# Cross-attention by pairs of token tiles, with maxima from stacked scores and a second, transposed score product

## What is computed

```python
q = einsum('bsd,hdk->bhsk', layernorm(x), Wq) + bq      # 16 heads, 16 wide
k, v = the same of ctx (2, 154, 256) with Wk, bk, Wv, bv
attn = softmax(q @ k.T / 4, axis=-1)                    # per head, 154 keys
x = x + concat(attn @ v) @ Wo + bo
logits = layernorm(x) @ router_w.T                      # 8 experts, the 2 best
x = x + sum over the 2 experts of w_e * gelu(xn @ w1[e].T) @ w2[e].T
```

## Time and profile before

| | us |
|---|---|
| median of 3 runs | 484.65 (482.76 to 489.57) |
| the profiled execution | 481.93, span 480.1 |
| PE busy | 421.6 (88%) |
| DVE, ACT, POOL busy | 327.6, 258.2, 259.8 |
| first scores of tile 0 | start at 17.78 |
| last logits copied (end of attention) | 207.45 |
| first expert product | starts at 236.93 |

### The profile page before, as it was taken

How to read it: one execution, slowest core, us unless ns; L and a number is a source line. 1 busy time by engine, 2 the same in 40 slices (tenths; PEclk the granted TensorE clock), 3 DMA queues, 4 the chain that set the end, 5 groups by cost and what they waited for, 6 DMA issues and landing times.

```text
span 480.1 us, 11162 instructions
## 1 busy us (share of the span) xinstructions
PE 421.6 (88%) x3421; PEld 373.5 (78%) x3422; DVE 327.6 (68%) x701; ACT 258.2 (54%) x509; POOL 259.8 (54%) x302
## 2 busy tenths in 40 slices
PE   7678999999999999722789999899999999999950
PEld 3467888888888887511489999899999999999940
DVE  1688999999999999569675755545446786664310
ACT  1555776677767775431076565454456767464410
POOL 2678778787777787410613364544544536462331
PEclk8999999999999999955799999999999999999995
DMA  8411111111111111075261734535324474232131
GB/s 235 143 40 46 57 56 67 56 77 65 55 55 61 59 56 67 23 202 173 58 259 48 219 56 122 132 51 128 50 42 129 90 223 91 39 59 34 24 38 12
DMA packets 24486, 41.98 MB, mean 87 GB/s; under 512 B 5952, under 2 KB 19136, under 8 KB 22400
## 3 DMA queue, kind: packets, MB, share of 16 engines
q1 hardware_dynamic: 13664, 28.68, 17.5%
q0 software_dynamic: 7296, 10.01, 12.2%
q10 hardware_dynamic: 3488, 2.83, 1.9%
HBM read 25.75 MB, written 9.45 MB: 73 GB/s over the span
## 4 chain that ended last, share of the span: by engine, by line
PE 73%; DVE 8%; DMA 7%; POOL 4%; issue 4%; ACT 1%; ACTq 1%; DVEq 0%; POOLq 0%
PE ps_s L1274 21%; PE ps_t L1291 13%; PE ps_s L1119 11%; PE ps_t L1294 7%; PE ps_t L1134 6%; PE ps_a L1152 3%; PE ps_c L1169 3%; DMA XS<-in_x 2%; PE ps_a L1075 2%; DMA result<-big,rowtok 2%; PE ps_a L1147 2%; DMA big<-rows,gtok 2%; PE ps_c L1256 2%; PE ps_c L1181 1%; PE ps_c L1175 1%
## 5 line engine op out<-in xcount | busy, mean ns | idle before, releaser
L488 POOL DMA_INDIRECT result<-big,rowtok x38 | 66.5, 1750 | 112.6 <-DMA result<-big,rowtok 63.2
L1274 PE MATMUL ps_s<-xgT,KB 128*128 128x256 f32 x912 | 116.0, 284 | 3.0 <-DVE xgT L999 3.0
L1274 PEld LDWEIGHTS ps_s<-xgT,KB 128*128 128x128 f32 x912 | 110.9, 191 | 4.1 <-DVE xgT L999 1.7
L1119 PE MATMUL ps_s<-KB 128*128 (+1 forms) x384 | 72.0, 324 | 9.4 <-DVE VP L756 3.2
L1119 PEld LDWEIGHTS ps_s<-KB 128*128 128x128 f32 x384 | 57.0, 193 | 14.3 <-issue 7.4
L456 POOL DMA_INDIRECT big<-rows,gtok x38 | 42.8, 1126 | 42.9 <-DVE gtok L976 23.7
L564 ACT ACTIVATE VP<-ps_t 128x512 f32<-128x512 f32 x80 | 47.5, 599 | 21.5 <-PE ps_t L1134 19.7
L393 POOL TENSOR_TENSOR half<-big 128x256 f32<-128x256 f32 x64 | 47.5, 742 | 16.2 <-ACT big L556 16.0
L1291 PE MATMUL ps_t<-KB,HTb 128*128 x160 | 56.0, 391 | 0.0
L646 ACT ACTIVATE big<-ps_t,wrow 128x256 f32<-128x256 f32 x38 | 18.1, 475 | 70.3 <-PE ps_t L1294 67.3
L1042 DVE SCALAR_TENSOR_TENSOR big<-ps_t,wrow,big 128x256 f32<-128x256 f32 x38 | 18.4, 483 | 52.4 <-ACT big L646 46.3
(11 more groups left out here) (159 smaller groups left out, 783.8 us busy)
## 6 DMA issues: line engine op xcount, KB each, us to landing
VP<-in_wexp SPq DMA_DIRECT2D x8, 1024.0 KB, 5.4
big<-in_wexp SPq DMA_DIRECT2D x8, 1024.0 KB
VP<-VP SPq DMA_DIRECT2D x16, 384.0 KB, 2.6
result<-x SPq DMA_DIRECT2D x16, 128.0 KB, 1.7
rows<-xn SPq DMA_DIRECT2D x16, 128.0 KB, 2.2
XS<-in_x ACTq DMA_DIRECT2D x1, 1536.0 KB, 11.9
big<-rows,gtok POOLq DMA_INDIRECT x38
result<-big,rowtok POOLq DMA_INDIRECT x38
```

What stands on the lines that cost most here:

```text
L488: pool.indirect_dma_start(out, bass.IndirectOffsetOnAxis(rowtok[:, u, h:h + 1], 0), ys[:, 2 * (u % 2) + h, :], None, compute_op=ALU.add).t ...
L1119: last = mm(ps_s[q % 2][:, j, 0:2 * KEYS].rearrange("p (h k) -> p h k", h=2), a[:, u, g, :], rhs, start=k == 0, stop=k == 2)
L1274: last = mm(ps_s[j // 4][:, j // 2 % 2, (j % 2) * PAIR:(j % 2 + 1) * PAIR], w1[:, w, k, j * P:(j + 1) * P], xgT[:, u % 2, a, k, :], start= ...
```

## The change

The attention goes over 8 pairs `m` of tiles, 256 tokens at a time, in steps from -3 to 9, all unrolled. In step `m` an engine makes the queries of pair `m+3`, the scores for the maxima of pair `m+1`, the second scores and exponentials of pair `m`, the values of pair `m-1`, and the router of pair `m-2`.

- **Stacked operands.** Two heads share an operand of 96 partitions: `KS` holds for each pair of heads high keys, high keys, low keys (32 partitions each), `QS` high, low, high queries. One matmul of 96 rows then gives what three gave. To move the parts onto these partitions, keys and queries go to DRAM (`kd`, `qd`: four transfers by SP) and come back (two by POOL, which also round to fp32r).
- **Maxima** are reduced from these scores (8 reductions of 616 columns a pair of tiles); the differences are no longer formed by DVE. The negated maxima, split into high and low (`nm`), are transposed on PE, moved to SBUF by ACT, written to DRAM (`md`) by SP and read into partitions 96 to 99 of `QS` by POOL.
- **Second product** (`turned_scores`): with 100 rows, keys as weights and 256 tokens streaming, it gives scores minus maxima with keys on the partitions. ACT takes the exponential straight from PSUM to `PTm`, `PTr`. There are no transposes of probabilities, no `evac_t`, no folds on POOL.
- **Values** (`value_sums`): a column of ones beside each head's values gives the sum of exponentials. The result is moved to SBUF, turned back (`back_transposes`), divided on DVE (`normalise`), turned again (`head_transposes`) and multiplied by `Wo`.
- Both layernorms' last step (`norm1`, `norm2`) moves from DVE to POOL.

The core of the diff, in the order SP, POOL, then the inner loops of PE's `scores`, `turned_scores` and `value_sums` (the setup, the tensors and the moved bookkeeping are left out):

```diff
+            def queries(m):
+                u = m % 3
+                if m >= 3:
+                    sp.wait_ge(qs_loaded[u], 32 * (m // 3))
+                sp.wait_ge(q_lo_made, m + 1)
+                for r in range(4):
+                    sp.dma_start(qd[u, :, :, 2 * r:2 * r + 2, :].rearrange("s l g n -> l s g n"),
+                                 Q2[32 * r:32 * r + 32, m % 2, :, :, :].bitcast(fp32)).then_inc(qd_stored[u], 16)
+            def maxima(m):
...
+                sp.wait_ge(nmT_made, m + 1)
+                sp.dma_start(md[u, :, :], nmT[:, :]).then_inc(md_stored[u], 16)
+            keys(0)
+            def step(m, has):
+                if has(3):
+                    queries(m + 3)
+                if m == -3:
+                    keys(1)
+                if has(1):
+                    maxima(m + 1)
...
+            def queries_read(m):
+                u = m % 3
+                pool.wait_ge(qd_stored[u], 64 * (m // 3 + 1))
+                if m >= 3:
+                    pool.wait_ge(g_psum, 10 * (m - 2))
...
+                pool.dma_start(QS[0:64, u, :, :], qd[u, :, :, :, :].rearrange("s l p n -> (s l) p n")).then_inc(qs_loaded[u], 16)
+                pool.dma_start(QS[64:96, u, :, :], qd[u, 0, :, :, :]).then_inc(qs_loaded[u], 16)
+            def maxima_read(m):
+                pool.wait_ge(md_stored[u], 16 * (m // 3 + 1))
...
+            for m in range(2):
+                rstd(m, mv1, var1_made, rstd1_made)
+                norm1(m)
+                if m == 0:
+                    keys_read(0)
...
+                pool.tensor_copy(KS[96:100, :, :, a * KEYS:(a + 1) * KEYS].rearrange("r b p k -> r (b p) k"),
+                                 own[96:100, a:a + 1].unsqueeze(2).to_broadcast([4, B * PAIRED, KEYS])).then_inc(ones_made, 1)
+            def step(m, has):
                 if has(-2):
+                    norm2(m - 2)
                 if has(0):
+                    maxima_read(m)
+                if has(2):
+                    queries_read(m + 2)
+                if has(3):
+                    low_queries(m + 3)
+                if m == -3:
+                    keys_read(1)
+                if m >= -2 and has(4):
+                    rstd(m + 4, mv1, var1_made, rstd1_made)
+                    norm1(m + 4)
                 if has(0):
+                    residual(m)
...
+                for j in range(2):
+                    p = 2 * k + j
+                    last = mm(ps_s[n % 2][:, j, 0:2 * KEYS], QS[0:96, u, p, i * P:(i + 1) * P],
+                              KS[0:96, m // (MACROS // B), p, :], start=True, stop=True)
...
+                for h in range(2):
+                    if j < 2:
+                        for p in (4 * j + 2 * h, 4 * j + 2 * h + 1):
+                            last = mm(bank[:, h, :], KR[0:100, b, p, :], QS[0:100, u, place(p), :],
+                                      start=p % 2 == 0, stop=p % 2 == 1)
+                    else:
+                        last = mm(bank[:, h, :], KS[0:100, b, place(j - 2), h * KEYS:h * KEYS + P],
+                                  QS[0:100, u, place(j - 2), :], start=True, stop=True)
...
+                for k in range(2):
+                    q = 2 * n + k
+                    mm(bank[:, k, :], V_rest[:, b, q, :], PTr[:, q, :], start=True, stop=True, skip_group_check=True)
+                    for j in range(4):
+                        last = mm(bank[32 * j:32 * j + 32, k, :], V_main[:, b, 4 * q + j, :], PTm[:, 4 * q + j, :],
+                                  start=False, stop=True, skip_group_check=True)
```

962 lines of the change are left out of this document (491 added, 471 removed).

## The result

The changed kernel takes **527.47 us** (median of 4 runs, 521.66 to 527.73) against 484.79 (482.76 to 489.57) of the kernel before in the same comparison: ratio 1.089, 95% interval 1.085 to 1.094. It is 9% slower, outside the forecast's range of 467 to 507 and beyond both slower rivals (510 and 512). The profiled execution has a span of 525.7 us.

What follows compares the result with a forecast made beforehand. It took PE as the bound, DVE 5% behind. Sums saved 42 us, but 12 went in the loop's waits and gaps and some 33 in start and end, so last logits came 2.6 later: 486 us, range 476 to 494 (outer 467 to 507).

Steps and rivals of the forecast that it cites:

- I take 0.5, nearer the memset: Price of one layernorm scaling on POOL, 256 columns: 0.5 us, between a memset's 0.33 and a two-input operation's 0.73.
- the walk: Dependency-ordered timing of one step, T being the start of turned_scores(m, 0): T repeats at 18.7 us, PE waiting about 1.
- the trip: The maxima's way from PE through ACT, SP's write to DRAM and POOL's read: landing at 18.4, setting the 18.7 us step.
- Landing of the read, 2.2: Time for POOL's read of the maxima to land after its 1.0 us issue, priced at 2.2 us.
- PE's sum of 16.3: PE's work for two tiles after the change, summed by operation prices: 16.3 us against 21.6 measured before.
- order of 17.7: PE's operations of one full step walked in order: back at turned scores 0 after 17.7 us.
- rival B: Trip hidden, leaving PE's order at 17.2 us a full step: last logits 13.5 us earlier, median 471; chance 0.28.
- value term: PE's value products: 1.15 us a quad, 4.6 a pair, including 0.15 per change of column grouping; bounds 3.4 and 8.4.
- rival D: Value blocks not side by side, or costlier switches: 8.4 us instead of 4.6, PE's order 21.5, total 512; chance 0.07.
- Step 0: First step, lacking values, heads and output: the maxima's way through DRAM is its longest loop, 15.6 us.
- The end: From the last pair's turned scores to the last logits: 26.2 us, with only the last router at the lower clock.
- C: Slower rival: each leg of the maxima's way through DRAM lands 1.2 us later, 24 in all, total 510; chance 0.25.

Runs made afterwards that it cites:

- Experiment 3: Changed kernel plus useless matmuls on PE where it stood idle ahead of turned_scores(m, 0): 513.18 us, ratio 1.063 to the kernel before.
- Experiment 5: Changed kernel with the queries' reads waiting for the maxima's read (525.05 us), the 256 KB store held back until that read landed (519.77), or both (514.08).
- experiment 1: Changed kernel with both layernorm scalings on DVE instead of POOL and rstd ahead of low_queries: 488.22 us, ratio 1.015 to the kernel before.
- experiment 7: Kernel with scalings on DVE and POOL's start reordered, plus SP writing maxima before queries: 473.95 us, repeated 474.83; then also with useless matmuls in PE's idle places: 479.8.
- experiment 9: Scalings on DVE, reordered start, maxima first, grouped value products, plus useless PE matmuls in the last pair: 468.95 us; earlier form, incomplete sum, fillers at start too: 472.43.
- experiment 2: Changed kernel with POOL issuing the maxima's read ahead of norm2 (506.23 us), or with only norm1 moved to DVE (508.41 us).

## Why the prediction was wrong, point by point

- **The step that failed: POOL's own order, and in it one term.** "I take 0.5, nearer the memset", with bounds of 0.33 and 0.73. A scaling takes 1.22; four a pair are 2.9 of the 3.1 us that POOL's chain is longer. With 0.5 the walk had POOL ready at T + 15.0 and the trip at 15.2, so it named the trip as what sets the step; with 1.22 it is POOL's chain. The bounds came from other operations (the lower one isn't even what the text says: 0.9 ns a column gives 0.23). The operation that moved has a row of its own in the kernel before, in the groups by line of DVE (20 to 220 us), and it was not used:

```profile
L715 DVE TENSOR_SCALAR xn<-x,mv 128x256 f32<-128x256 f32 x16 | 12.7, 792 | 2.4 <-POOL mv L372 2.4
```

  That is 0.79, above my upper bound already; by it the wait would have been about 1 us longer a step. But this row would have been right by luck. Its 0.79 is not DVE's own price: the timeline of the kernel before shows the operation at 0.80 to 0.82 in 30 of 32 cases (with `norm1`, the same operation), each beside one of POOL's two-input operations, and at 0.41 in the two with none beside them:

```profile
103.20 0.74 POOL L393 TENSOR_TENSOR half<-big 128x256 f32<-128x256 f32 x1
103.27 0.82 DVE L715 TENSOR_SCALAR xn<-x,mv 128x256 f32<-128x256 f32 x1
...
204.91 0.41 DVE L715 TENSOR_SCALAR xn<-x,mv 128x256 f32<-128x256 f32 x1 [0.67 <-POOL mv L372]
```

- **The clock was left out of the walk.** I forecast a wait of 1 us in each step and priced everything behind it at full clock. Behind the waits of 3.5, 4.2 and 4.1 us PE ran at 1.2 GHz for some 11 us (granted clock 0.54 to 0.58; router 1.71 for 0.96, four turned scores 1.05 for 0.64 to 0.74). It did so behind shorter ones too, 1.8 at T(7), and 2.2 at T(2) with `norm1` on DVE, but not behind the two of 2.0 there. Experiment 3 prices this at 14 of the 42 us, 10.5 of them up to T(7).
- **Landing of the read, 2.2, measured 4.5 to 5.2 at m = 2 to 4.** The value was that of the gathers; with no store beside it (m = 0 and 1) the read took 2.9. The store that it meets is triggered by `norm2`, which stood right ahead of the read on the same engine; I priced both and did not ask what the one sets off. Experiment 5: 1.0 to 1.6 us a landing, 6.4 us at T(7) and 9 at the last logits, from one execution; it takes more than the store, and what more isn't shown. These three are not to be added up: each wait lowers the clock and so lengthens the next.
- **PE's sum of 16.3 and order of 17.7** (17.2 in rival B, which doesn't fit the walk). A full step without waits is 18.3 (experiments 1 and 7). The value term was right: 4.6, of which the change of grouping 0.165 for the 0.15 taken from the earlier trace rows; by that rival D, with 21.5 for the order, is out. But the change does not double these switches, as the prediction says: a tile had five (from 128 to 64, 32, 64, 32 and 128 columns), a pair has eight, and ten with the maxima's transposes (32 columns), so there are no more per token than before. Too small were a group of scores, 0.39 from start to start for 0.28, and an exponential, 0.60 on ACT for 0.50, which paces turned 7 to 9. So the full step of 18.7 came out as 18.3 once POOL was free, but by PE's order and not, as forecast, by the trip, whose read then landed 0.4 us ahead of PE. The floor that rival B counted on, 17.2, was not there. Step 1 has no router and took 17.1; the walk counted it as full. **Step 0** took 18.1 for 15.6, with a clock of 0.65 in its first half; with PE filled ahead of it (experiment 7) it was 15.9.
- **The start** was walked well: scores of pair 0 at 44.8 (44), T(0) 63.9 (61.5). Some parts cancelled: a copy into `KS` 2.24 (2.9), an issue on POOL 0.5 to 0.65 (1.0), scalings 2.44 a pair (1.0). Its last sentence, that scores at 30 would make it case B, was half right: with scores at 29.3 the kernel is 6.7 us under the one before, not 13.5.
- **Steps 5 and 6**: 16.7 and 16.8 (16.1). **The end**: 36.2 (26.2). With the scalings on DVE (experiment 1) it is 30.4, of which the last scalings themselves are 1.7 (2.43 on POOL, 0.74 on DVE); with fillers too (experiment 9) it is 26.4. So the walk was right for full clock, with the last router at half clock, where two thirds of the end ran so (granted clock 0.66). How much of it does varies between kernels whose end is the same: 31.1 to 36.2 us at clocks of 0.83 to 0.66 in the changed kernel and experiments 2, 3 and 5. One profile each can't price anything in the end to better than some 3 us.
- **Rivals.** C had the right sign and in the main the wrong mechanism: the read was issued 3 us late by POOL's arithmetic, besides landing 2 to 3 us late. Theory 2 of experiment 1, which is C, fell. The case that happened, POOL's order as the bound, stood in the walk (15.0 against the trip's 15.2, a tie) but had no rival of its own and no price for being wrong; with both bounds of 0.33 and 0.73 it moved by less than 1 us and seemed safe.

## What to carry to other kernels

Price an operation that moves to another engine by the row that it has where it stands, undisturbed, times what that engine needs for a like operation, and never by a cheaper kind of operation. Even this gives a lower bound only: two inputs of 256 columns take 0.42 on DVE and 0.73 on POOL, which makes 0.7 out of 0.41, and 1.22 was measured. Where the new engine has no row for the same form, the upper bound is open, and a small run that times it comes first. When a walk ends in a tie between two loops, the term with the least evidence in either is a rival. And where the walk shows a wait on PE of some microseconds in each step, walk the step again with everything behind it at half clock.

## What the runs showed of the hardware

- POOL takes 1.22 us for 128 x 256 with two operations and two scalars per partition, 1.07 with constants, 0.93 with one operation; DVE takes 0.41 for the first (403 to 415 ns for `norm2` in experiment 1).
- The same DVE operation took 0.80 to 0.82 in the kernel before beside POOL's two-input operations and 0.41 without one. In the kernels with the maxima first, too, two of DVE's scalings take 1.69 when one of POOL's two-input operations runs beside them, and 0.73 when none does:

```profile
107.55 1.69 DVE L737 TENSOR_SCALAR xn<-XS,mv 128x256 f32<-128x256 f32 x2
...
107.74 1.35 POOL L413 TENSOR_TENSOR KB<-qf,KB 128x512 fp32r<-128x512 f32 x1 [3.09 <-ACT KB L573]
...
114.16 0.73 DVE L747 TENSOR_SCALAR xn<-x,mv 128x256 f32<-128x256 f32 x2
```

  Beside POOL's operations with one input and one column (0.38 us, at 204.97 in the kernel before) the 0.41 stayed.
- A transfer of 32 KB landed in 1.4 to 3.6 us with no store issued right behind it (the reads in 2.8 or more); with a store of 256 KB issued 0.08 us behind it the landing took 3.4 to 5.2.
- In two of the profiled executions one gather of the experts' part made PE wait 5.0 us, which is as much as several of the effects measured here.
